# Query stage of a perceiver kernel: key products moved half a pair behind the query products, second fold moved ahead of the second half's query products

## What is computed

```python
def _L0_xattn_ref(hidden_q, kv_c, Wq, w_kc_q, w_kc_kv, W_qr, W_kr, Wo):
    H, K, D_C, D_CQ, R = (16, 128, 64, 192, 64)
    q_hk = (hidden_q @ Wq.T).reshape(Bv, Sv, H, K)
    q_big = jnp.einsum('bshk,hkq->bshq', q_hk, w_kc_q)
    q_big = _apply_rope(q_big, sin_q[None, :, None, :], cos_q[None, :, None, :])
    kv_r = _apply_rope(kv_c, sin_k[None], cos_k[None])
    q_r = jnp.einsum('bshq,hqr->bhsr', q_big, W_qr)
    k_r = jnp.einsum('bld,hdr->bhlr', kv_r, W_kr)
    scores = jnp.einsum('bhsr,bhlr->bhsl', q_r, k_r)
    attn = jax.nn.softmax(scores, axis=-1)
    ctx_c = jnp.einsum('bhsl,bld->bhsd', attn, kv_r)
    ctx_lat = jnp.einsum('bhsd,hkd->bhsk', ctx_c, w_kc_kv)
    ...
    return ctx @ Wo.T
```

## Time and profile before

| | us |
|---|---|
| median of 3 runs | 1531.56 |
| lowest and highest | 1529.84, 1533.69 |
| the profiled execution, its own time | 1534.25 |
| its span in the trace | 1532.2 |
| query stage: pair 0 begins at | 17.49 |
| pair 7 begins at | 153.52 |
| last DMA issues of the stage begin at | 175.58 |

### The profile page before, as it was taken

One profiled execution on the slowest core, in us unless ns is written; L12 is line 12 of the kernel. 1 busy time (PEld: TensorE's weight loads), 2 busy tenths in 40 slices (PEclk: granted clock), 3 DMA queues, 4 the chain that ended last, 5 costly groups with the idle time before them and its releaser, 6 DMA issues. The chain is left out here.

```text
span 1532.2 us, 32593 instructions
## 1 busy us (share of the span) xinstructions
PE 1410.4 (92%) x13504; PEld 975.6 (64%) x13504; DVE 1094.2 (71%) x1710; ACT 603.4 (39%) x1012; POOL 611.5 (40%) x935
## 2 busy tenths in 40 slices
PE   6888689999997878999999999999999878999999
PEld 3444368877895455676776667676666664665556
DVE  5778486588547777988889998889899635444443
ACT  3334254345433534554455555445555321111110
POOL 1200143244314646577666657766656710000000
PEclk9999899999999898999999999999999989999999
DMA  8444300110000131222222222122112105000000
GB/s 225 153 123 112 76 1 1 29 29 1 1 1 1 32 79 34 45 45 55 50 59 45 55 45 50 50 50 59 44 43 51 36 17 221 1 1 0 14 1 14
DMA packets 125955, 74.63 MB, mean 49 GB/s; under 512 B 95536, under 2 KB 107056, under 8 KB 124016
## 3 DMA queue, kind: packets, MB, share of 16 engines
q1 hardware_dynamic: 125808, 72.55, 18.1%
HBM read 54.68 MB, written 17.83 MB: 47 GB/s over the span
## 5 line engine op out<-in xcount | busy, mean ns | idle before, releaser
L1879 DVE SCALAR_TENSOR_TENSOR W<-PS,wc,W 128x504 f32<-128x504 f32 x375 | 271.1, 732 | 40.0 <-ACT W L1572 30.9
L2209 PE MATMUL PS<-HT,wgu 128*128 128x512 f32 x320 | 143.5, 592 | 0.0
L1572 ACT ACTIVATE W<-PS,wc 128x512 f32<-128x512 f32 x125 | 86.0, 688 | 138.3 <-PE PS L1273 86.5
L1273 PE MATMUL PS<-HT,wv 128*128 128x512 f32 x252 | 121.5, 614 | 8.5 <-DVE W L1879 8.5
L2343 DVE SCALAR_TENSOR_TENSOR act<-th,PS 128x512 f32<-128x512 f32 x48 | 33.0, 687 | 128.9 <-ACT th L2269 128.9
L1460 PE MATMUL PS<-wo,ogT 128*128 128x256 f32 x512 | 117.5, 388 | 7.7 <-DVE dl L1950 5.1
L1273 PE MATMUL PS<-HT,wkq 128*128 128x512 f32 x248 | 118.1, 620 | 3.0 <-DVE W L1879 3.0
L1296 PE MATMUL PS<-wz,HT 128*128 128x256 f32 x512 | 120.3, 387 | 0.0
L1460 PEld LDWEIGHTS PS<-wo,ogT 128*128 128x128 f32 x512 | 99.5, 195 | 22.4 <-DVE dl L1950 5.3
L2269 ACT ACTIVATE th<-PS 128x512 f32<-128x512 f32 x48 | 28.7, 597 | 206.5 <-PE PS L2209 206.5
L1296 PEld LDWEIGHTS PS<-wz,HT 128*128 128x128 f32 x512 | 94.9, 191 | 17.5 <-issue 4.0
(11 more groups left out here) (277 smaller groups left out, 2952.1 us busy)
## 6 DMA issues: line engine op xcount, KB each, us to landing
a_rows<-AT SPq DMA_DIRECT2D x16, 512.0 KB, 3.1
wk<-in_l0x_k SPq DMA_DIRECT2D x16, 384.0 KB, 3.7
wgu<-in_moe_gu SPq DMA_DIRECT2D x5, 1024.0 KB, 16.4
queries_scratch<-tts SPq DMA_DIRECT2D x32, 128.0 KB, 2.8
wkq<-in_gdn_w SPq DMA_DIRECT2D x16, 256.0 KB, 3.2
wv<-in_gdn_w SPq DMA_DIRECT2D x16, 256.0 KB, 2.8
wz<-in_gdn_w SPq DMA_DIRECT2D x16, 256.0 KB, 2.8
wo<-in_gdn_w SPq DMA_DIRECT2D x16, 256.0 KB, 3.0
```

The source lines that it names most:

```text
L1273: mm = pe.matmul(PS[:, qbank(h, q), :], w[:, o:o + DK], HT[:, k, f * 512:(f + 1) * 512], start=(k == 0), stop=(k == DC - 1))
L1572: a.activation(acc[:, flows(h, q), :], PS[:, qbank(h, q), :], ACT.Copy, scale=wc[:, h % 2, 4 * c + 3:4 * c + 4]).then_inc(s["tap"], 1)
L1879: v.scalar_tensor_tensor(a0, p0, wc[:, h % 2, 4 * c + 2 - k:4 * c + 3 - k], a0, ALU.mult, ALU.add).then_inc(s["conv"], 1)
L2209: mm = pe.matmul(PS[:, 2 * (i % 2) + w, :], pack[:, k, w, :], HT[:, k, f * N:(f + 1) * N], start=(k == 0), stop=(k == DC - 1))
```

## The change

PE's order in the loop becomes: queries 0; first fold of the next pair; `fold_pair` of the next pair; keys 1 of the pair before; second fold of the next pair; queries 1; keys 0. The last keys 1 comes behind the loop. Within `queries` the tile t = 2 goes first, and the wait for `ts0` or `ts1` stands behind it, as keys never write that bank. `fold_pair` gets a wait of its own for the second weight load (`w1`), because the second fold now comes later.

ACT's order follows: swap 0, evict the first fold, keep keys 1 of the pair before, evict `fold_pair`, evict the second fold, swap 1, keep keys 0. DVE does `latent` between its two ropes instead of behind them. SP issues the two loads ahead of store 0 instead of behind it, and each load waits in addition for the fold that reads the buffer (`cf`).

```diff
                     if h > 1:
                         sp.wait_ge(s["wf"], h // 2)
+                        sp.wait_ge(s["cf"], h - 1)
...
                     ahead(u)
-                    store(u, 0)
                     if u + 2 < PAIRS0:
                         load(2 * u + 4)
                         load(2 * u + 5)
+                    store(u, 0)
...
                 def fold_pair(u):
+                    pe.wait_ge(s["w1"], u * 32 + 32)
                     if u > 0:
                         pe.wait_ge(s["ws"], u)
...
                     if u == 0:
                         pe.wait_ge(s["hT"], 4 * f + 4)
-                    else:
-                        pe.wait_ge(s[f"ts{f}"], u)
-                    for t in range(3):
+                    for t in (2, 0, 1):
+                        if u > 0 and t == 0:
+                            pe.wait_ge(s[f"ts{f}"], u)
...
-                    queries(u, 1)
                     if u + 1 < PAIRS0:
                         fold(2 * u + 2)
-                    keys(u, 0)
+                        fold_pair(u + 1)
+                    if u > 0:
+                        keys(u - 1, 1)
                     if u + 1 < PAIRS0:
                         fold(2 * u + 3)
-                        fold_pair(u + 1)
-                    keys(u, 1)
+                    queries(u, 1)
+                    keys(u, 0)
+                keys(PAIRS0 - 1, 1)
...
                     swap(u, 0)
-                    swap(u, 1)
                     if u + 1 < PAIRS0:
                         folded(2 * u + 2)
+                    if u > 0:
+                        keep_keys(u - 1, 1)
+                    if u + 1 < PAIRS0:
+                        folded_pair(u + 1)
+                        folded(2 * u + 3)
+                    swap(u, 1)
                     keep_keys(u, 0)
-                    if u + 1 < PAIRS0:
-                        folded(2 * u + 3)
-                    keep_keys(u, 1)
+                keep_keys(PAIRS0 - 1, 1)
...
                     rope(u, 0)
-                    rope(u, 1)
                     if 1 <= u <= 6:
                         latent(u - 1)
+                    rope(u, 1)
                     if 4 <= u <= 6:
                         butterfly(u - 4)
```

More of the change, by code:

```diff
@@ L357, in folded, with folded_pair @@
                                  PS[:, 0, 0:DC * CQ].rearrange("p (k t n) -> p k t n", k=DC, t=3), ACT.Copy).then_inc(s["cs"], 1)
[L358 to L361, removed]
+                def folded_pair(u):
+                    a.wait_ge(s["wf"], u + 1)
+                    a.activation(mw[:, u % 2, :, :], PS[:, 1, 0:3 * DCTX].rearrange("p (t n) -> p t n", t=3), ACT.Copy).then_inc(s["ms"], 1)
+                    a.activation(W2[:, u, :], PS[:, 1, D:2 * D], ACT.Copy).then_inc(s["ws"], 1)
                 def swap(u, f):
@@ L383, in _ @@
                 folded(1)
+                folded_pair(0)
                 for u in range(PAIRS0):
```

## The result

The changed kernel takes 1518.87 us, median of 6 runs (1516.5 to 1520.86), against 1531.99 for the kernel before (6 runs, 1529.84 to 1535.9). The ratio is 0.9917, with a 95% interval from 0.9896 to 0.9938: faster by 13.1 us, clear of the 0.3% that a measurement can tell. The forecast was 1525.2, in a range from 1514.5 to 1531.0. The measured time is within 0.3 us of what the first rival gave (1518.6, "POOL comes just late"), and the trace says that this is what happened. That the total agrees so closely is partly luck: by the last store of the stage that rival gives 6.4 + 6.6 = 13.0 us, and the trace shows 11.8; the rest of the measured gain lies behind the stage.

The account below looks back on a forecast made before the run. PE was taken as the busiest engine, 16.16 of 18.10 us a pair, idle 1.94. Pair 7 starting 9.3 us earlier, less a 2.9 us longer tail, gives 6.4 us: 1525.2 against the median 1531.56, range 1514.5 to 1531.

Parts of the forecast that it names:

- the first rival: Pair 2: `ug` starts over 0.5 us later against the rope, only the last `rot` is held; 6.6 us better, chance 0.26.
- The normal pair: PE's waits of 0.92 us (eviction) and 1.02 us (rope) go; period 16.2 us, saving 1.9 a pair.
- the new wait of 0.16 us for the copied keys: In a normal pair, PE's tile 2 ends at E+12.55 but the bank is free at E+12.71.
- Pair 0: Gains little: `fold_pair` needs the last weight load, landed at 29.8; pair 1 starts at 38.4 against 38.81.
- or 2.5 us of idle in pair 0 bring the clock down: Part of the rival that waits change places: PE's clock falls in pair 0, 3 us; that rival's chance 0.12.
- The rival of late loads: Weight loads of pairs 3, 4 and 7 land late and stop PE; at 4 us late, 1540 us; chance 0.07.
- So POOL is first by 0.5 us: Pair 2: POOL starts `ug` at E+13.3, `rf` at E+13.77, so `rf` and the last `rot` are both held.
- E: The moment at which queries 0 of a pair end on PE, from which the prediction counts its times.
- Only one DVE instruction is long: Sign of being wrong, against `rf` and the last `rot` of pair 2 both near 4.5 to 5 us.
- fold is released by a DMA beyond pair 0: Sign of being wrong: a fold or `fold_pair` on PE waits for a DMA in a pair after pair 0.
- The tail: From pair 7's start to the last store: 2.9 us longer, keep keys 0 at 16.0 behind the start against 13.0.
- the case with POOL first: The forecast case: two DVE instructions held, PE waits 5.6 us, pair 3 takes 24.8 us; gain 6.4 us, chance 0.52.

Follow-up runs that it names:

- Experiment 4: Changed kernel with the query tiles back in the old order 0, 1, 2; 1532.44 us in a single run.
- experiment 2: Changed kernel with SP's order of before, store 0 ahead of the two loads; 1543.16 us in a single run.
- experiment 1: Changed kernel with the DMA of `ug` issued 1.3 us earlier, ahead of the stores of half 1 of pair 1; 1518.4 us in a single run.
- experiment 7: Changed kernel with context transfers behind the loads of pair 1 and the twelve early transfers behind pair 5's loads; 1523.37 us, ratio 0.9949.
- Experiment 3: Changed kernel with POOL's two scalings cut to one column, `ug` and `dn` left unscaled; last store at 159.47 instead of 163.76 us.
- experiment 10: Changed kernel, second fold and `fold_pair` behind queries 1, POOL's scalings in quarters: 1514.17 us; with pair 5's loads ahead of early transfers too: 1516.77 us.

## Why the prediction was right or wrong

**The normal pair: right.** Both waits went, as worked out. The period was 15.98 instead of 16.2: the new wait of 0.16 us for the copied keys does not show on PE, only on its weight loads. Experiment 4 shows that it was rightly seen as the one that takes over: 1.73 us if tile 2 is not first.

**Pair 0: wrong by 1.5 us.** The weight load landed 8.2 us behind its issue at 21.51, as taken. What I left out is the clock. PE stood still for 2.77 and 0.54 us, and from 30.20 ran at the 1.2 GHz level for 3.2 us (PEclk 0.50):

```profile
28.32 0.92 PE L285 MATMUL PS<-wk 128*128 128x192 f32 x4 [2.77 <-DMA wr<-in_l0x_r]
29.77 0.71 PE L296 MATMUL PS<-wr 64*64 64x64 f32 x12 [0.54 <-DMA wr<-in_l0x_r]
...
30.20:33.40 3.20, 3.20 (x15) 2.17 (x12) 0.23 (x1) 0.85 (x3) 0.00 (x0) 0.50 0.67 238
```

I had it only in a rival, "or 2.5 us of idle in pair 0 bring the clock down", at 3 us; it cost about half of 3.2. Pair 1 started at 39.88, not at 38.4. The rival of late loads put the clock's fall at a wait past about 3.5 us; the runs show it behind shorter ones too (2.77 and 0.54 here, 2.12 and 0.42 in experiment 2).

**Pair 3: the step that failed** is "So POOL is first by 0.5 us". Three terms stand in it. `ug` was issued 5.31 us behind E (61.12 to 66.43), where the terms gave 5.4. `rf` began at E+13.58, where I had 13.77. And from issue to POOL's start it took 8.63 us, where I had taken 7.87 from the one row of the kernel before. That term alone turned the sign. What follows from the sign was right: with POOL first I had 24.8 us for the pair, and experiments 1 and 7 measured 22.57 and 24.53; with POOL late I had 6.6 us less, and the measured 17.53 is 7.3 less than 24.8. (By the prediction's own terms it should read 6.8: 5.6 + 3.0 less 1.2 and 0.6. The 0.6 for the next rope did not show.) "Only one DVE instruction is long" and "fold is released by a DMA beyond pair 0" were written down as signs of being wrong, and both came. The traces side by side, POOL's start less that of `rf`:

| kernel | POOL less `rf`, us | held | pair 3, us |
|---|---|---|---|
| experiment 1 | -0.87 | `rf` and `rot` | 22.57 |
| experiment 2 | -0.54 | `rf` and `rot` | 21.24 (loads late as well) |
| experiment 7 | -0.07 | `rf` and `rot` | 24.53 |
| experiment 4 | -0.01 | `rot` | 17.89 (period 17.90) |
| before (pair 2) | +0.30 | `rot` | 24.22 (pair 2) |
| changed, second profile | +0.32 | `rot` | 17.53 |
| changed, first profile | +0.36 | `rot` | 17.53 |
| changed, third profile | +0.50 | `rot` | 17.53 |

That two instructions in a row would each be held was only inferred in the prediction; it is shown by experiments 1, 2 and 7. The sentence of the Trainium skill (SBUF — State Buffer, section Who interferes with whom) that the order of issue decides agrees with seven of the eight lines. In the line of experiment 4 the two starts lie too close to say which was issued first; that `rf` was not held and POOL took 0.4 us longer fits `rf` being first. Why the landing took 8.1 to 8.7 us in all changed kernels and 7.8 in the one trace before is open: not the loads behind it (experiment 2, 8.4), nor the stores ahead of it (experiment 1, 8.6, where it is issued ahead of them).

**Pair 6: missed.** The rival of late loads was there in small. `wr` landed 6.3 us behind its issue at 121.34, behind the twelve early transfers, and PE waited 0.95 and 0.18 us; the pair took 17.45 instead of 16.2. Putting the loads first removes it (15.99 in experiment 7). I had a landing 1 to 2 us ahead of the fold, by shorter landings. The rival's premise, that loads can turn the change into a loss, is what experiment 2 shows, with another cause.

**The tail: right.** 2.9 us longer was forecast, and 24.96 less 22.06 is 2.90; keep keys 0 at 15.94 against 16.0. Experiment 3 splits it: 1.27 by POOL, the rest by the order.

**The sum.** For the last store the case with POOL first gave a gain of 6.4 us; it was 11.8. Of the 5.4 between, pair 3 makes 7.3, the four normal pairs 0.9, pair 0 takes back 1.5 and pair 6 1.3: 5.4. So nearly half of what the stage gained over its pairs (6.7 of 14.7 us) would mostly be gone with POOL first, as experiments 1 and 7 show, and the forecast had that the other way. In the kernel before POOL was behind `rf` as well: the same one held `rot` made PE wait 4.18 us there and brought the clock down, and 1.32 us now, as keys 1 come later and have slack. The chances were fair for the sign (faster at 0.67), and the range held because the rival was in it. But a margin of 0.5 us at the end of a chain of 13 us, with one transfer's landing in it, was no ground for giving the forecast twice the chance of its rival.

## What to carry to other kernels

When two engines exclude each other, ask first who comes first, and by what margin; if a DMA landing is in the chain, treat both outcomes as even, or make the question harmless by cutting the blocking engine's work into pieces shorter than the slack of the chain it blocks (in the tail of experiment 10, where there was little slack, the pieces gained nothing). A reorder on one engine shifts such meetings elsewhere: experiment 7 improved two stretches by 4 us, lost 7 in a third and 3 more in two others. And take a change apart: here without the order of three tiles most of a pair's gain was gone, two loads moved ahead of a store on the DMA queue kept the change from being a loss, and the second fold's new place cost more than it gave.

## What the runs showed of the hardware

A 128x512 DVE instruction with both inputs in SBUF, 0.68 us alone, took 4.4 to 5.0 when a 128x2048 POOL instruction had begun 0.07 to 0.87 us ahead of it; begun 0.30 to 0.50 us ahead of POOL it was not slowed. Further into a POOL instruction the hold was shorter (2.1 to 2.9 us), and the held instruction ended about 0.55 us behind POOL's (0.54 to 0.56 in the changed kernel and experiment 1). Two in a row each waited for one POOL instruction (experiments 1, 2 and 7). The DVE instructions of the rope that read PSUM stayed at 0.7 in all these traces. POOL's pieces of 128x512 held a single one to 0.8 to 1.8 us, and POOL took 11.4 to 12.6 us for the same work instead of 9.6. The landing of one and the same 2 MB transfer varied from 7.8 to 8.7 us, and that of a 64 KB weight load in pair 0 of experiment 7 from 2.9, issued first, to 10.4, issued behind the context. The granted clock fell to 0.50 behind a wait of 2.32 us in one trace and stayed at 1.00 behind one of 2.48 in another.
